# Twelve-head sums issued by source block, expert results gathered earlier, next layer's weights in pieces, output stored as 120 and 5 rows

## The reference

```python
x = x + gnn0(norm(x), src, dst)   # three attention layers: 12 heads of 64, 12 heads of 64, 1 head of 768
x = x + moe0(norm(x))             # 8 experts of inner width 256, two per node, gates rebalanced
x = x + gnn1(norm(x), edges)      # two attention layers: 4 heads of 512, 1 head of 768
x = x + moe1(norm(x))             # 8 experts of inner width 384, two per node, biases b1 and b2
```

## Time and profile before

| | |
|---|---|
| time, median of 3 runs | 3344.09 us (3337.66 to 3348.24) |
| the profiled execution's own time | 3337.54 us |
| its span, mean granted clock | 3335.8 us, 0.925 |
| busy: PE, PEld, DVE, ACT, POOL | 2911.3, 2159.9, 1936.9, 1125.0, 131.9 us |
| m0, first to last expert product | about 1744 to 1910 us |
| m1, first expert product to the end | about 3031 to 3336 us |

### The profile page before, as it was taken

One profiled execution on the slowest core, in us unless ns is written; L12 is line 12 of the kernel. 1 busy time (PEld: TensorE's weight loads), 2 busy tenths in 40 slices (PEclk: granted clock), 3 DMA queues, 4 the chain that ended last, 5 costly groups with the idle time before them and its releaser, 6 DMA issues.

```text
span 3335.8 us, 45466 instructions
## 1 busy us (share of the span) xinstructions
PE 2911.3 (87%) x14693; PEld 2159.9 (65%) x14694; DVE 1936.9 (58%) x3777; ACT 1125.0 (34%) x1815; POOL 131.9 (4%) x187
## 2 busy tenths in 40 slices
PE   6867799998959999986969759979999997987994
PEld 4544688887548888854657624458888564566772
DVE  6757999985699999546541124477652334632113
ACT  1111577775237777621113301122110220211110
POOL 0000000000000000000001120000000000000112
PEclk9989799998969999988979979989999999987995
DMA  2000111111011111100125642122213110022434
GB/s 69 0 33 25 54 51 59 50 38 51 0 55 47 46 52 53 47 6 16 61 70 172 201 145 83 47 72 73 78 61 125 47 48 18 33 101 96 166 137 148
DMA packets 80302, 227.85 MB, mean 68 GB/s; under 512 B 13983, under 2 KB 26729, under 8 KB 77555
## 3 DMA queue, kind: packets, MB, share of 16 engines
q1 hardware_dynamic: 57641, 163.81, 13.6%
q0 software_dynamic: 16144, 47.16, 4.8%
q10 hardware_dynamic: 6400, 15.36, 1.3%
HBM read 174.59 MB, written 54.43 MB: 69 GB/s over the span
## 4 chain that ended last, share of the span: by engine, by line
PE 38%; DVE 6%; DMA 5%; issue 2%; ACT 1%; SPq 0%; POOL 0%; ACTq 0%; DVEq 0%; POOLq 0%
PE psum L1096 15%; PE psum L968 10%; PE psum L1224 4%; PE psum L1233 4%; PE psum L1063 2%; DMA arena<-y_rows,arena 1%; DVE arena L1678 1%; DMA arena<-xn_rows,arena 1%; DMA y_rows<-arena 1%; PE psum L1172 1%; DVE arena L2014 1%; DVE arena L1801 1%; PE psum L1206 1%; PE psum L1211 1%; DMA arena<-raw 0%
## 5 line engine op out<-in xcount | busy, mean ns | idle before, releaser
L968 PE MATMUL psum<-arena 128*125 128x384 f32 (+1 forms) x1776 | 642.3, 521 | 7.7 <-ACT arena L1336 7.7
L1126 PEld LDWEIGHTS psum<-arena 125*125 125x125 f32 x4800 | 581.0, 191 | 59.0 <-DVE arena L1812 8.7
L1126 PE MATMUL psum<-arena 125*125 (+1 forms) x4800 | 566.9, 271 | 6.0 <-DVE arena L1812 6.0
L968 PEld LDWEIGHTS psum<-arena 128*125 128x125 f32 x1776 | 333.4, 190 | 289.8 <-issue 115.0
L1096 PE MATMUL psum<-arena 125*125 125x256 f32 (+3 forms) x2040 | 511.1, 412 | 4.8 <-DVE arena L1862 4.2
L1096 PEld LDWEIGHTS psum<-arena 125*125 125x125 f32 x2040 | 382.7, 188 | 123.2 <-DVE arena L1862 4.5
L1116 PE MATMUL psum<-arena,spread 126*125 126x313 f32 (+1 forms) x1304 | 430.6, 454 | 33.8 <-DMA arena<-r_rows 18.0
L1812 DVE SCALAR_TENSOR_TENSOR arena<-arena,edge_counts 125x625 f32<-125x625 f32 x480 | 383.2, 807 | 66.4 <-ACT arena L1424 65.8
L1411 ACT ACTIVATE arena<-arena,el 125x625 f32<-125x625 f32 x464 | 373.8, 806 | 0.8 <-DMA arena<-el_rows 0.8
L1745 DVE CUSTOM_DVE_ANT_0 arena<-arena,no_edge_bias 125x1250 bf16<-125x1250 f32 x250 | 363.9, 1456 | 6.0 <-DMA arena<-el_rows 2.5
L1424 ACT ACTIVATE arena<-psum,el 125x625 f32<-125x625 f32 x326 | 255.0, 782 | 214.0 <-PE psum L1116 198.6
(11 more groups left out here) (217 smaller groups left out, 2698.3 us busy)
## 6 DMA issues: line engine op xcount, KB each, us to landing
arena<-el_rows SPq DMA_DIRECT2D x49, 610.4 KB
arena<-in_L_ffn_W SPq DMA_DIRECT2D x16, 1152.0 KB, 8.9
y_rows<-arena SPq DMA_DIRECT2D x47, 384.0 KB, 2.4
arena<-r_rows SPq DMA_DIRECT2D x22, 610.4 KB
arena<-in_L_w SPq DMA_DIRECT2D x16, 768.0 KB, 6.2
arena<-in_L_gnn_W SPq DMA_DIRECT2D x4, 3072.0 KB, 14.4
raw<-arena POOLq DMA_DIRECT2D x38, 250.0 KB, 2.8
arena<-raw SPq DMA_DIRECT2D x8, 1000.0 KB
```

Of the source, the lines that this page charges most:

```text
L968: ins = e.matmul(bank[0:P, 0:w], L.xt[u][:, k, :], L.w_sb[:, k, at:at + w], start=(k == 0), stop=(k == L.KT - 1))
L1126: ins = e.matmul(banks[2 + half][0:P, d * 65:(d + 1) * 65], Ph[half][:, s, d * P:(d + 1) * P], L.z[:, s, h, :], start=(s == 0), stop=(s == ...
```

## The change

- **Twelve-head layers.** `sum_tile` becomes `sum_block`: one call adds one source block s to all five target tiles, four steps after that block's step (BEHIND = 4). Since five sums are open at once in one bank, a one-row bf16 matmul of 325 columns opens the bank in place of five start flags. The one-element matmul and `p_free` go; `ag_ready` takes their place for DVE and SP. `finish` moves to steps 5 and 15.
- **m0.** The arena is laid out anew, so that row blocks 0, 1 and 3 of g3's projection are loaded at the start of m0, block 2 after expert 0, half of block 4 after expert 1, the vectors after expert 2 and the rest after expert 6. Expert 1's weights are loaded when the routing is listed.
- **Results.** The two slots of a node are ordered, so that pick 0 is in the earlier expert. The pick-0 results of six tiles are gathered when all tiles ahead of the last expert are stored; the others follow in a fixed order through a ring of six single buffers.
- **m1.** b2 is loaded with an expert's weights, broadcast to 128 rows, and added when DVE copies a result out. The gate turns, their products and the DVE adds go. A tile's output is stored as 120 and 5 rows, even tiles from SP and odd ones from ACT.

```diff
-YG = 3
+YG = 6
+ROWS = 120
+OUTPUTS = ([(0, t) for t in range(YG)] + [(1, 0), (1, 1), (1, 2), (0, 6), (1, 3), (0, 7), (1, 4), (0, 8), (1, 5), (0, 9)]
+           + [(1, t) for t in range(6, T)])
+BEHIND = 4
...
+        def store_rows(e, M, t):
+            for lo, hi in ((0, ROWS), (ROWS, P)):
+                e.dma_start(by_tile(M.dst)[lo:hi, t, :], M.acc[lo:hi, t, :]).then_inc(M.stored, 16)
+
         def moe_sync(e, M, following):
             def load_w(x, u):
...
+                if M.bias:
+                    e.dma_start(M.b2s[u], over(A["L1_ffn_b2"][x, :], ST)).then_inc(M.w_in[u], 16)
...
+            def load_piece(k, lo, hi):
+                rows = slice(k * 128, (k + 1) * 128)
+                e.dma_start(following.w_sb[:, k, lo:hi], following.W[rows, lo:hi]).then_inc(following.w_in[k // 3], 16)
+
             load_w(0, 0)
+            if following is not None:
+                for k in (0, 1, 3):
+                    load_piece(k, 0, following.F)
+                e.wait_ge(M.listed, 1)
             load_w(1, 1)
             e.wait_ge(M.placed, 1)
-            if M.bias:
-                e.dma_start(M.b2, A["L1_ffn_b2"]).then_inc(M.b2_in, 16)
...
-            store_outputs(EX - 2)
-            if following is not None:
-                load_vectors(e, following)
-                e.wait_ge(M.w_free, EX - 1)
-                apart(e)
-                load_projection(e, following, 1)
-            store_outputs(EX - 1)
-            if following is not None:
-                n = all_tiles(e, M)
-                e.wait_ge(M.w_free, EX)
-                e.wait_ge(M.y_out, 16 * n + 16)
-                apart(e)
-                e.wait_ge(M.xg_sb, n + 1)
-                apart(e)
-                load_projection(e, following, 0)
+            for x in range(EX):
+                store_outputs(x)
+                if x < EX - 2:
+                    e.wait_ge(M.w_free, x + 1)
+                    apart(e)
+                    load_w(x + 2, x % 2)
+                if following is None:
+                    continue
+                if x == 0:
+                    load_piece(2, 0, following.F)
+                elif x == 1:
+                    load_piece(4, 0, following.F // 2)
+                elif x == 2:
+                    load_vectors(e, following)
+                elif x == 6:
+                    e.wait_ge(M.w_free, EX - 1)
+                    apart(e)
+                    load_piece(4, following.F // 2, following.F)
+                    load_piece(5, 0, following.F)
+            if following is None:
+                for t in range(0, T, 2):
+                    e.wait_ge(M.y_done, t + 1)
+                    store_rows(e, M, t)
+                e.wait_ge(M.stored, 32 * T)
+                return
...
-            e.wait_ge(L.p_free, L.since["p_free"] + 2 + 2 * L.H - 1)
+            if L.batched:
+                e.wait_ge(L.ag_ready, L.since["ag_ready"] + 2 * L.H - 1)
+            else:
+                e.wait_ge(L.p_free, L.since["p_free"] + 2 + 2 * L.H - 1)
             load_projection(e, following, 0)
...
-            e.wait_ge(M.y_out, 16 * n + 16)
+            last = e.value_load(M.span[0:1, EX - 1:EX], min_val=1, max_val=MAX_TILES)
+            e.wait_ge(M.y_out, 16 * last + 16)
             apart(e)
-            for t in range(T):
-                if t >= YG:
-                    e.wait_ge(M.y_done, t - YG + 1)
-                for k in range(2):
-                    at = bass.IndirectOffsetOnAxis(ap=M.slot_i[:, k * T + t:k * T + t + 1], axis=0)
-                    e.indirect_dma_start(M.yg[t % YG][k], None, y_rows[:, :], at).then_inc(M.yg_in[t % YG], 16)
+            for m, (k, t) in enumerate(OUTPUTS):
+                if m == YG:
+                    e.wait_ge(M.y_out, 16 * n + 16)
+                    apart(e)
+                if m >= YG:
+                    k0, t0 = OUTPUTS[m - YG]
+                    if k0:
+                        e.wait_ge(M.y_done, t0 + 1)
+                    else:
+                        e.wait_ge(M.yg_free, T * M.before + t0 + 1)
+                at = bass.IndirectOffsetOnAxis(ap=M.slot_i[:, k * T + t:k * T + t + 1], axis=0)
+                e.indirect_dma_start(M.yg[m % YG], None, y_rows[:, :], at).then_inc(M.yg_in[m % YG], 16)
...
-            def sum_tile(h, half, d, part):
-                if d == 0 and part == 0:
+            def sum_block(h, half, s):
+                if s == 0:
                     e.wait_ge(L.out_done, L.since["out_done"] + 2 * h + half + 1)
-                if d == 0:
-                    e.wait_ge(L.p_ready, L.since["p_ready"] + 4 + 2 * T * h + half * T + (part + 1) * HT)
-                for s in range(part * HT, (part + 1) * HT):
+                    e.matmul(banks[2 + half][0:P, 0:HT * 65], nil.to_broadcast([1, P]), nil.to_broadcast([1, HT * 65]),
+                             start=True, stop=False)
+                e.wait_ge(L.p_ready, L.since["p_ready"] + 4 + 2 * T * h + half * T + s + 1)
+                for d in range(HT):
                     ins = e.matmul(banks[2 + half][0:P, d * 65:(d + 1) * 65], Ph[half][:, s, d * P:(d + 1) * P], L.z[:, s, h, :],
-                                   start=(s == 0), stop=(s == T - 1))
-                if d == HT - 1 and part == 1:
+                                   start=False, stop=(s == T - 1 and d == HT - 1))
+                if s == T - 1:
                     ins.then_inc(L.ag_ready, 1)
-                    e.matmul(banks[1][0:1, 0:1], ident[:, 0:1], ident[:, 0:1], start=True, stop=True).then_inc(L.p_free, 1)
 
             def batched_head(h, u, first, last):
                 for j in range(2 * T):
-                    half, s = j // T, j % T
                     if not vector_block(h, j):
                         exponents(h, j)
-                    if not (first and half == 0):
-                        sum_tile(h if half else h - 1, 1 - half, s // 2, s % 2)
+                    if j >= BEHIND:
+                        sum_block(h, (j - BEHIND) // T, (j - BEHIND) % T)
+                    elif not first:
+                        sum_block(h - 1, 1, T + j - BEHIND)
...
-                for d in range(HT):
-                    for part in range(2):
-                        sum_tile(L.H - 1, 1, d, part)
+                for s in range(T - BEHIND, T):
+                    sum_block(L.H - 1, 1, s)
...
-            if M.bias:
-                n = all_tiles(e, M)
...
-                    for c in range(2):
-                        ins = e.matmul(banks[4 + 2 * (t % 2) + c][0:P, 0:C // 2], M.gt[t % 2], M.b2[:, c * (C // 2):(c + 1) * (C // 2)],
-                                       start=True, stop=True)
-                    ins.then_inc(M.gb_ready, 1)
...
-                    if not first and j in (1, T + 1):
-                        finish(h - 1, j // T)
+                    if not first and j == BEHIND + 1:
+                        finish(h - 1, 1)
+                    if j == T + BEHIND + 1:
+                        finish(h, 0)
...
-                finish(L.H - 1, 0)
                 finish(L.H - 1, 1)
...
+        def add_outputs(e, M, t):
+            lo = OUTPUTS.index((1, t - 1)) + 1 if t else 0
+            for m in range(lo, OUTPUTS.index((1, t)) + 1):
+                k, own = OUTPUTS[m]
+                e.wait_ge(M.yg_in[m % YG], 16 * (M.before * -(-(2 * T - m % YG) // YG) + m // YG + 1))
+                a = M.acc[:, own, :]
+                if k:
+                    e.wait_ge(M.yg_free, T * M.before + own + 1)
+                ins = e.scalar_tensor_tensor(out=a, in0=M.yg[m % YG], scalar=M.gate[k][:, own:own + 1], in1=a, op0=ALU.mult, op1=ALU.add)
+                ins.then_inc(M.y_done if k else M.yg_free, 1)
...
+                for c in range(2):
+                    o, src = M.y[:, c * (C // 2):(c + 1) * (C // 2)], banks[2 + c][:, 0:C // 2]
+                    if M.bias:
+                        ins = e.tensor_tensor(o, src, M.b2s[u][:, c * (C // 2):(c + 1) * (C // 2)], ALU.add)
+                    else:
+                        ins = e.tensor_copy(o, src)
+                ins.then_inc(M.y_sb, 1)
```

More of the change, by code:

```diff
@@ L238, in __init__ @@
         self.y_out = s("y_out")
[L239 to L245, removed]
+        self.loads = 48 if bias else 32
+        self.yg_in, self.yg_free, self.before = yg_in, yg_free, before
         self.y_done = s("y_done")
@@ L272, in graph_transformer @@
         small = sb("small", [128, 256])
+        nil = small[0:1, 160:161].bitcast(BF16)[:, 0:1]
         ARENA = 38400
@@ L1530, in graph_vector @@
             st.add(e.memset(zero, 0.0))
+            st.add(e.memset(small[0:1, 160:161], 0.0))
             for w in range(2):
@@ L1806, in weights @@
                 half, s = j // T, j % T
[L1807 removed]
+                if s == 0 and not L.batched:
                     e.wait_ge(L.p_free, L.since["p_free"] + 2 * h + half + 1)
+                elif s == 0 and not (isinstance(h, int) and h == 0):
```

(15 more changed lines are left out.)

121 lines of the change are left out of this document (51 added, 70 removed).

## The result

The changed kernel takes 3282.43 us (median of three; 3281.95 to 3290.72) where the kernel before took 3344.09: a ratio of 0.983, interval 0.980 to 0.986. Timed again with six more runs it is at 3281.65, ratio 0.984 (0.981 to 0.987). So it is faster by 62 us between medians, and by 55.1 us between the two profiled spans (3335.8 and 3280.7), on which the rest of this text works. The forecast was 80 between profiled executions and 3258. The time lies inside the 80% range, 3240 to 3290, but above the forecast's own, 3240 to 3276, where the rivals stood.

A forecast was written before the change was run, and what follows sets the result against it. PE was taken to bound the steady twelve-head layers, and transfers, gathers and stores the layer ends, m0 and the tail. Terms -22.0 + 1.4 - 28 - 31.8 = -80.4 from 3337.5 gave 3257, stated as 3258 us; 80% range 3240 to 3290.

The forecast's parts named there:

- the forecast's own: Whole kernel: the range 3240 to 3276 us in which the forecast itself holds, given a chance of 0.59.
- signs of being wrong: Listed beforehand: PE idle before a block's sums, a 12 us gather in the tail, a stall over 10 us in experts 3 to 6.
- 786 KB over 401 GB/s: m0: block 2 goes behind expert 2's weights, costed at +1.5 us with something lost.
- the +1.4 for both layers: Twelve-head layers: net cost in us of 48 opening matmuls at 0.22, less the one-element matmuls at 0.19 a half.
- The upper bound, 10.6: Twelve-head layers: highest cost allowed for the opening matmuls, 48 x 0.22 us, with nothing credited for those that go.
- Between 0 and 16 us I take 3: m0: stall of the experts by the vectors' 16 us load, taken as 3 us.
- the rival of 0.12: m0: the vectors stall the experts for all their 16 us; m0 gains 15, about 3270; chance 0.12.
- Its "against": m0: claimed that nine of the vectors' sixteen us are left when the next store comes, and only five engines are held.
- the forecast's steps make 34: m0 to g3: quicker gathers, stores and one add fewer start g3 at 1922.8, 34.3 us earlier, before 6.2 of costs.
- the rival of 0.15: Tail: gathers bound it in three rounds of 13.6 us; 16 gained in place of 32, about 3273; chance 0.15.
- +1.3: Tail: cost in us of loading b2, 384 KB, with each expert's weights; bounds 0 and 2.4.
- The slow rival: Twelve-head layers: PE waits for each block; at 0.25 us a step 120 lost, about 3377; chance 0.04.

## Why the prediction was right, and by how much it was off

The direction was right, and all three places won; no rival of the slow side came. The rest was right in part. The sum was 25 us too good (80.4 forecast, 55.1 measured), so that the time came out where the forecast had put its rivals, and m0, forecast to win more than the layers, won least. One of its own signs of being wrong came as well: a stall over 10 us in expert 3 (DVE waited 15.37 us for the store). Two steps of its working do not follow from their numbers, but move little: 3257 raised by 0.2% is 3264 and not 3258, and 786 KB over 401 GB/s are 2.0 us and not 1.5.

- **Twelve-head layers: 14.5 won, 20.6 forecast.** The mechanism holds: SP starts after step 13's block, the bias is no longer waited for, and from the last exponents to the next layer 11.3 us are won in g0 and 10.3 in g1, where 11.0 were forecast. The step that failed is the price of the opening matmul, which makes the +1.4 for both layers 4.3 a layer, 8.7 in all. It was put at 0.22 us from the busy time of a bf16 row of 416 columns. It takes 0.357, near that row's single duration (0.361) and not its share when such matmuls follow one another. The upper bound, 10.6, held it. What remains of the 14.5, 1.6 us, lies ahead of the steady layers, where profiles differ by more than that.
- **m0 to g3: 11.2 won, 28 forecast.** The step that failed is "Between 0 and 16 us I take 3". The vectors cost the middle of m0 10.5 us against before, 8 to 11 by the run that takes them out of it. That was the rival of 0.12, whose 15 us for m0 is near 11. Its "against" failed twice. Only five engines are held, but stores run on those engines as well, and `M.y` is one buffer. And more than nine microseconds were left when the store came: the transfer, put at 16 us from its issue, stood behind weights on the queue, and the store, issued ten microseconds behind the vectors, landed 25 us after them. The first gather cost 3.3 and not 1.7 (the first activation is 15.1 us behind that gather's start, 11.8 before), and the tiles up to the sixth 2.0 where block 2 was put at 1.5. The hand-over itself, from the last activation to the projection, fell by 27 us where the forecast's steps make 34: the last gather of rows waited 1.4 us and no longer 6.62, as foreseen, but the early gathers took 10.13 us beside the pieces, the last store came late, and the pair's gather took 6.94 and not 3.8.
- **Tail: 26.7 won, 31.8 forecast.** Thirteen issues took 23.2 us (1.78 each), not 19.6, in a stretch where the engines were full (0.99), and the last gather landed after 8.36, not 6: the rival of 0.15, gathers that bound the tail, is partly true. b2 cost 0.4 us against +1.3.
- **Not foreseen:** some 3 us more are won elsewhere, 2.4 of them between g3's first projection and m1's first gather. No run here takes that apart, and the other profile of the changed kernel differs by nearly 2 us there.
- **The slow rival** is answered by the runs: 5.7 us of waits in all, a clock of 1.00 and PE at 100% in 500 to 600, and 4.4 us a layer more at half the distance.

What stays open is how the vectors could be had for less than about 8 us: no run with the vectors among the experts has a middle under 124.0, against 116.5 without them. Loading them before the routing is done was not tried, since their place in memory is still in use then.

## What to carry to other kernels

A transfer that is moved out of one stage is paid for in the stage that it is moved into: there, count which engines it holds, for how long, and what with a single buffer has to pass through the same engines, and take that stall whole unless a row shows otherwise. Cost a new small instruction by the duration of one, not by its share in a run of many. Where a tail is bound by transfers, spreading them over all engines was worth 16 us and starting some early 11, and after that nothing more came from starting more of them earlier.

## What the runs showed of the hardware

- Loading one 8 KB row of DRAM to 125 partitions moved 131 GB/s at a share of 0.31; loading it to 120 partitions, with a gather and a store beside it, kept the engines at a share of 0.90 for 214 GB/s, where the fullest stretch of the kernel before moves 401 at 1.06. More engines for such a load did not make it faster in proportion.
- A bf16 matmul of one row over 325 columns took 0.357 us, about as long as one of 125 rows over 416 columns (0.361), and taking 24 of them out of a layer made it 9.8 us shorter, 0.41 each.
- PE work put into idle time of the first head ran at a granted clock of 0.60: more busy time (13.54 us of 20 against 6.84) came with no higher clock in that stretch (0.65 before).
